# Zero matmuls in the open sums of TensorE, and new orders on all engines, in a four-block token tower on one core

## The chip, the cores and the metric

The kernel runs on one NeuronCore of one Trainium2 chip. Its time is the device time of one launch in microseconds. A NeuronCore has five engines that run side by side, each through its own list of instructions: TensorE (PE, matmuls into PSUM), VectorE (DVE), ScalarE (ACT, table functions such as exp and gelu), GpSimd (POOL), and SyncE (SP, here the issuer of nearly all DMAs). They wait for each other by semaphores, and none of them may overtake in its own list.

## The reference, cut to what matters

64 sequences of 128 token ids go through a tower. Activations are rows of 128 features; all arithmetic is float32.

```python
h = token_block(x)                       # embedding + layer norms, ffn, 8-head attention (second of two layers), ffn
h = h + mamba_block(layernorm(h))        # forward and backward selective scan over time, then ffn and layer norms
h = h + moe(layernorm(h))                # router, 8 experts of gelu(x @ w1[e] + b1[e]) @ w2[e], top 2 combined
h = h + attention(layernorm(h))          # 8 heads
h = h + nibble_alu(layernorm(h))         # rounded features, small relu networks, one-hot outputs
# the scan, for each of 2 directions and each of 16 state indices:
#   h_t = exp(dt_t * A) * h_(t-1) + (dt_t * u_t) * B_t ;  y_t += h_t * C_t
```

## The kernel before

Four sequences form a group: 512 columns (4 x 128 time steps) with the 128 features on partitions. There are 16 groups. On each engine the work of a group is cut into four streams, each a Python generator that stops (`yield`) after every small item:

- `P` (`token`, line 429 in the PE block): the token block and its layer norms, in PSUM banks `bank_p`.
- `A` (`scan`): the selective scan, 32 states of a group (16 forward, 16 backward). For one state ACT computes `decay` (exp), POOL computes `dbu` (dt*u times a row of B), DVE runs two scan instructions into PSUM `states` (L921), two multiplications with the row of C (L927) and two additions into `y_sum` (L932). SP loads the two broadcast rows.
- `C` (`middle`): what follows the scan: the projection back, an ffn, two layer norms, the router, and 8 experts. An expert is 4 times a matmul `h` into `bank_a` (L569), a gelu on ACT, and a matmul `y` that adds to a sum in `bank_b` (L580). The sum is open from the first `y` to the fourth; then DVE takes it out (L1106). The ffn before the experts uses `bank_b` in the same way (L538).
- `D` (`beside`): the preparation of both scan directions of the next group (`pre`), and the last layer of the group two before (`last_layer`), in `bank_c`.

So four groups are in flight at once, at different stages. In which order an engine takes items of the four streams is written out by hand as a string of letters for each engine, in the table `ORDER` (lines 42 to 170), and `drive` (line 348) walks it: each letter takes the next item of that stream. The work inside each stream has a fixed order; only the interleaving is in the strings. Items of a group in the middle of the run repeat the same letters from group to group in the version before (about 218 us apart).

Every f32 matmul of the source is two PE instructions in the profile (1,024 of L569 are 512 matmuls), each with its own weight load. ACT holds one table set at a time: exp and ln share one, gelu, tanh-gelu and silu have one each. `af` (line 697) asks for the exp set when it changes to it (that load has line L701 in the profile); the other loads stand in front of the activation (L705). How often the set changes follows from the letters alone.

Of the kernel before, what the change touches and what calls it, by code (L numbers as in the profile page):

```python
# [14 lines left out]
NSEQ, L, D = 64, 128, 128  # L15
# [34 lines left out]
        "PCCDCCPCCDPPDPCCPCCDPPDCCPPCCPCCCCDCCPCCDPDCCCCDCCDPDPDPCCPCCDDDCCPCCPPCCPPCCPPCCPCCPPDCCDCCDDPCCPDC"  # L50
        "CDCCPPCCDCCDDPCCDPPPCPCCPCDPDCPPCCCCDDCCDCPPDCDDPPDCDDDCDDCDDCDDDDDCCCPCCDPPCCDDPDPCCPDPCCDPCCDCCPCC"
        "DPPDPPPCCCCDCCPCCDPDDPCCCCPCCDCCPDDPDCCCCPCCDPCCPDPPCCPPCCPCCPPDCCDDPCCDCCPDCCDCCPPCCDCCDDPCCDPPPCPC"
        "CPCDPDCPPCCCCDDCCDCPPDCDDPPDCDDDCDDCDDDCDCCCDCCPDDPPCCPDCCDCPCCCPDDPCCPDPCCDCCDCCPCCPDPPDCCPPDCCPDCC"
        "DCCDCCDCPCCCPDDPCCPCCDDDPCCPCCPPPCCPPCCPCCPPDCCDDCCDPCCDCCDCCPPCCDDPDDPPCPCCPPCPCDPCCDCCPPDDPCCDCPPP"
# [1433 lines left out]
```

How the kernel before makes its waits and increments, by code:

```python
    def link(eng, ins, name):  # L298
        eng.wait_ge(s[name], tick(ins, name))
# [17 lines left out]
        @block.tensor  # L318
        def _(pe):
            pe.wait_ge(done["w"], 16)
            pe.wait_ge(done["cols"], 16)
            for i, (name, a, b) in enumerate(FOLD):
                nc.tensor.matmul(A[:, i:i + 1], w(name, a=a, n=128), col(b), start=True, stop=True).then_inc(done["b"], 1)
            pe.wait_ge(done["s"], 1)
            for i in range(2):
                nc.tensor.matmul(B[:, i:i + 1], w(f"wo{i}"), small[:, i:i + 1], start=True, stop=True).then_inc(done["c"], 1)
# [1 line left out]
        @block.vector  # L328
        def _(dve):
            dve.wait_ge(done["b"], len(FOLD))
            nc.vector.tensor_copy(small[:, 0:2], A[:, 0:2]).then_inc(done["s"], 1)
            nc.vector.tensor_copy(COLT[:, COL["q0"]:COL["q0"] + 2], A[:, 2:4])
            b1 = COLT[:, COL["tb1_00"]:COL["tb1_00"] + 2 * NF]
            nc.vector.tensor_tensor(b1, A[:, 4:4 + 2 * NF], b1, ALU.add)
            nc.vector.tensor_scalar(w("tw2_1"), w("tw2_1"), 0.5, None, ALU.mult)
            for name, g in (("wqk0", "tl1s1"), ("wqk1", "tl1s1"), ("wv1", "tl1s1"), ("tw1_0", "tl2s0"), ("tw1_1", "tl2s1")):
                nc.vector.tensor_scalar(w(name), w(name), col(g), None, ALU.mult)
            dve.wait_ge(done["c"], 2)
            nc.vector.tensor_copy(COLT[:, COL["c0"]:COL["c0"] + 2], B[:, 0:2]).then_inc(done["fold"], 1)
            dve.wait_ge(done["fold"], 1)
```

## Time and profile before

| | |
|---|---|
| median of 3 runs | 3891.53 us (3889.09 to 3901.82) |
| the profiled execution's own time | 3896.18 us |
| its span, first to last instruction | 3893.9 us |
| mean granted TensorE clock | 0.887 of full |

The span is what all rows below refer to; 2.3 us lie around it. A row of a group of instructions gives their count, their busy time in all, the mean of one, and the idle time that the engine had just in front of them. Granted clock 1.00 means that TensorE ran at its upper level (2.4 GHz), 0.50 at its lower one (1.2 GHz) in the whole stretch, and values between are mixtures of both.

### The profile page before, as it was taken

The numbers are of one execution on the slowest core, as the hardware profiler recorded it, in microseconds if no ns is written. First come the engines' busy times: TensorE is split into PE (matmuls) and PEld (weight loads), VectorE is DVE, ScalarE is ACT, GpSimd is POOL, SyncE is SP. The second block draws the span as 40 slices with busy tenths as digits, with TensorE's granted clock in tenths as the row PEclk, the third lists the DMA queues.
The fourth block names the chain that finished last, engine by engine and source line by source line (L and its number), as shares of the span: only waits on it lengthen the run. The fifth ranks groups of instructions, "written<-read, shape, count | busy, mean of one in ns | idle before, by whom it ended". The sixth has DMA issues, their size and how long they took to land.

```text
span 3893.9 us, 31221 instructions
## 1 busy us (share of the span) xinstructions
PE 3127.3 (80%) x8728; PEld 1368.3 (35%) x8728; DVE 3420.1 (88%) x4654; ACT 2925.3 (75%) x3806; POOL 1337.2 (34%) x644
## 2 busy tenths in 40 slices
PE   5655878889787788979888888979788887877797
PEld 3231423334343333424343333424343333432232
DVE  1499979999898999999999999999999998999822
ACT  2546887987868888787888878787888879686442
POOL 0254333333323334343433443343433433333200
PEclk8757788989888899989999999989989999888797
DMA  1233333424324243333434342343424333333310
GB/s 63 77 108 96 113 109 92 128 80 135 99 94 118 93 131 95 119 118 109 125 98 123 107 131 94 121 117 109 124 95 126 104 116 104 104 119 104 100 49 11
DMA packets 209022, 404.60 MB, mean 104 GB/s; under 512 B 25936, under 2 KB 34256, under 8 KB 208592
## 3 DMA queue, kind: packets, MB, share of 16 engines
q1 hardware_dynamic: 206800, 398.41, 32.8%
q0 software_dynamic: 2048, 4.20, 1.0%
q8 instruction: 69, 1.13, 0.1%
q14 instruction: 105, 0.86, 0.1%
HBM read 387.57 MB, written 14.94 MB: 103 GB/s over the span
## 4 chain that ended last, share of the span: by engine, by line
PE 37%; DVE 26%; ACT 25%; issue 12%; POOL 0%; DMA 0%; DVEq 0%; ACTq 0%; POOLq 0%
PE bank_a L569 8%; DVE states L921 7%; PE bank_b L580 7%; ACT L705 6%; DVE states L927 6%; ACT decay L705 6%; DVE y_sum L932 3%; ACT L701 3%; ACT tok L705 3%; ACT last L705 3%; ACT middle L705 3%; PE bank_p L478 1%; PE bank_c L397 1%; PE bank_p L421 1%; PE bank_c L640 1%
## 5 line engine op out<-in xcount | busy, mean ns | idle before, releaser
L1199 POOL TENSOR_TENSOR dbu<-dtu,b_rows 128x1024 f32<-128x1024 f32 x512 | 1243.4, 2431 | 2104.1 <-DVE states L921 1823.6
L921 DVE TENSOR_TENSOR_SCAN states<-decay,dbu 128x512 f32<-128x512 f32 x1024 | 1298.7, 1311 | 38.1 <-ACT decay L705 30.5
L705 ACT ACTIVATE decay<-dt,neg_a 128x508 f32<-128x508 f32 x1024 | 659.4, 707 | 64.6 <-DVE states L921 59.0
L705 ACT ACT_TABLE_LOAD x516 | 662.0, 1283 | 47.5 <-PEq L344 16.6
L569 PE MATMUL bank_a<-middle,experts 128*128 128x512 f32 x1024 | 616.2, 687 | 97.1 <-ACT middle L705 88.9
L705 ACT ACTIVATE middle<-bank_a,columns 128x512 f32<-128x512 f32 x608 | 417.8, 687 | 329.6 <-PE bank_a L569 305.4
L927 DVE TENSOR_TENSOR states<-states,c_rows 128x512 f32<-128x512 f32 x960 | 610.8, 679 | 0.3
L932 DVE TENSOR_TENSOR y_sum<-y_sum,states 128x512 f32<-128x512 f32 x960 | 609.9, 674 | 0.2
L580 PE MATMUL bank_b<-middle,experts 128*128 128x512 f32 x1024 | 572.7, 643 | 21.4 <-ACT middle L705 11.8
L705 ACT ACTIVATE last<-bank_c 128x512 f32<-128x512 f32 (+2 forms) x320 | 201.0, 634 | 198.0 <-PE bank_c L617 52.4
L701 ACT ACT_TABLE_LOAD x232 | 297.7, 1283 | 46.0 <-PE bank_p L469 17.0
L580 PEld LDWEIGHTS bank_b<-middle,experts 128*128 128x128 f32 x1024 | 209.2, 208 | 312.0 <-issue 248.1
L569 PEld LDWEIGHTS bank_a<-middle,experts 128*128 128x128 f32 x1024 | 187.5, 209 | 365.5 <-issue 189.5
L705 ACT ACTIVATE tok<-bank_p,columns 128x512 f32<-128x512 f32 x304 | 203.7, 684 | 64.9 <-PE bank_p L421 36.7
L397 PE MATMUL bank_c<-xin,weights 128*128 128x512 f32 x256 | 151.9, 687 | 94.6 <-DVE xin L1018 55.8
L705 ACT ACTIVATE tok<-bank_p 128x512 f32<-128x512 f32 x224 | 132.3, 590 | 100.2 <-PE bank_p L376 47.7
L421 PE MATMUL bank_p<-tok,weights 128*128 128x512 f32 x256 | 153.2, 683 | 56.9 <-DVE tok L896 35.1
L1106 DVE SCALAR_TENSOR_TENSOR middle<-bank_b,columns,comb_rows 128x512 f32<-128x512 f32 x128 | 94.8, 741 | 117.0 <-PE bank_b L580 115.7
L426 PE MATMUL bank_p<-tok,weights 128*128 128x512 f32 x256 | 147.4, 660 | 51.2 <-ACT tok L705 51.1
L478 PEld LDWEIGHTS bank_p<-tok 128*128 128x128 f32 x1024 | 150.0, 218 | 98.1 <-ACT tok L705 64.3
L478 PE MATMUL bank_p<-tok 128*128 128x17 f32 x1024 | 147.8, 279 | 36.3 <-ACT tok L705 36.0
L379 PE MATMUL bank_p<-tok,weights 128*128 128x512 f32 x128 | 83.0, 734 | 58.2 <-ACT tok L705 57.5
(206 smaller groups left out, 3944.7 us busy)
## 6 DMA issues: line engine op xcount, KB each, us to landing
b_rows<-bc_scratch SPq DMA_DIRECT2D x512, 256.0 KB, 3.4
c_rows<-bc_scratch SPq DMA_DIRECT2D x512, 256.0 KB, 3.3
experts<-ew SPq DMA_DIRECT2D x128, 512.0 KB, 3.5
comb_rows<-comb_scratch SPq DMA_DIRECT2D x128, 256.0 KB, 3.8
h_scratch<-tok SPq DMA_DIRECT2D x16, 256.0 KB, 3.3
x_scratch<-xin SPq DMA_DIRECT2D x16, 256.0 KB, 3.8
xr<-x_scratch SPq DMA_DIRECT2D x16, 256.0 KB, 4.9
h<-h_scratch SPq DMA_DIRECT2D x16, 256.0 KB, 5.3
```

Source lines behind the costliest of these rows:

```text
L397: last = mm(bk, w(dn + "in", a=128 * e, n=128), xin[:, :], start=True, stop=(e >= HALVES))
L421: tick(mm(bh, w(w1, a=128 * c, n=128), x, start=True, stop=True), p + "h")
L426: tick(mm(by, w(w2, a=128 * (c - 1), n=128), slots[c - 1], start=(c == 1), stop=(c == NF)), p + "y")
L478: last = mm((P, Q)[hd // 4][:, at:at + 17], ex[:, it % 2, blk(2 * i + j)], va[:, 2 * a + j, hd, :], start=True, stop=True)
L569: tick(mm(A, EW[:, e % 2, 128 * c:128 * c + 128], s_xn, start=True, stop=True), "e_h")
L580: tick(mm(B, EW[:, e % 2, FF + 128 * c:FF + 128 * c + 128], gbuf[:, k % 4], start=(c == 0), stop=(c == NF - 1)), "e_y")
L701: act.preload_act_table_set("natural_log_exp_and_others")
L705: return nc.scalar.activation(out, in_, func, **more)
L921: tick(nc.vector.tensor_tensor_scan(hs[:, h, ::step], da[:, n % DECAYS, h, ::step], dbu[:, n % AHEAD, h, ::step], 0.0, ALU.mult, ALU.add), ...
L927: tick(tt(hs[:, h] if st else y_sum[:, h], hs[:, h], c_rows[:, n % SLOTS], ALU.mult), "a_hc")
L932: tick(tt(y_sum[:, h], y_sum[:, h], hs[:, h], ALU.add), "a_y")
L1199: tick(nc.gpsimd.tensor_tensor(dbu[:, n % AHEAD], dtu[:, k % 2], row, ALU.mult), "a_dbu")
```

## The change

Three things change.

1. The five strings of `ORDER` are replaced by new ones. Counts of P, A, C and D are as before on every engine (PE 753 P, 1,282 C, 801 D; ACT 2,261 letters; DVE 2,823; POOL 546; SP 1,317). The new strings don't repeat from group to group.
2. The string of PE has 1,435 letters `F` besides. Each is one bf16 matmul of 256 columns: weights that are all zero, a moving operand read twice from the first 128 columns of the constant tile `selections`, added (`start=False, stop=False`) to columns 0 to 255 of `bank_b`. Every `F` stands after an item of `C` that leaves a sum in `bank_b` open. They wait for nothing and signal nothing.
3. A tile of zeros takes 256 bytes of each partition; one `memset` on DVE fills it in the set-up. To make room, `neg_a` has no tile of its own, but is computed in place in `weights`.

```diff
 ORDER = {
     "passes": 0,
     "PE": (
-        "PDCPPPPPPPPPPPPCPPPPPPPPPPPPPPPPPPPPPPPPPPPPPPPPPPPDDDPDCPDPDPPDDPDDPPDPPDPPPPPPPPPPPPPPPPPPPPPPPPPP"
+        "PDCPPPPPPPPPPPCPPPPPPPPPPPPPPPPPPPPPPPPPPPPPPPPPPPPDDPDDPCDPDPDDPPDDPPDPPDPPPPPPPPPPPPPPPPPPPPPPPPPP"
+        "PPPPPPPPPPPDDDPDDPDPPDDPPPPPPPPPPPCPCPDDCFFFFFFFFFFFFFFFFFFFCCPFDCCDCCPPFFFFFPPFFFFPPFFFFFCCPCPCPPPC"
...
-    NEGA = sb("neg_a", [128, 2 * HALVES * DS])
+    ZERO = sb("zeros", [128, 128], BF16)
     EW = sb("experts", [128, 2, 2 * FF])
+
+    NEGA = W[:, AT["falog"][0]:AT["falog"][0] + 2 * HALVES * DS]
...
         def _(dve):
+            nc.vector.memset(ZERO[:, :], 0.0)
             dve.wait_ge(done["b"], len(FOLD))
...
-            drive("PE", P=each(token), C=whole(fold, middle), D=beside())
+            def nothing_added():
+                finite = sel("fieldcum").rearrange("p (a t) -> p a t", a=1).to_broadcast([128, 2, 128])
+                for _ in range("".join(ORDER["PE"]).count("F")):
+                    mm(B[:, 0:256].rearrange("p (s t) -> p s t", s=2), ZERO[:, :], finite, start=False, stop=False)
+                    yield
+
+            drive("PE", P=each(token), C=whole(fold, middle), D=beside(), F=nothing_added())
```

What the new strings say when they are counted:

| | before | after |
|---|---|---|
| changes of ACT's table set that the letters cause | 747 | 669 |
| runs of `F` on PE, and the longest | - | 328, 30 |
| `F` in runs of 10 or more | - | 677 in 40 runs |
| `F` from the middle stream of group 15 on | - | 22 |
| DVE items after the last `A` | 52 D, 26 C | 53 D, 26 C |
| scan states issued on POOL before the gathers of groups 2, 3, 4 | 63, 94, 127 | 57, 88, 119 |

## Rows read from the trace of the kernel before

**Rows 1.** The page: busy us, share of the span, instructions; granted clock in fortieths.
```profile
PE 3127.3 (80%) x8728; PEld 1368.3 (35%) x8728; DVE 3420.1 (88%) x4654; ACT 2925.3 (75%) x3806; POOL 1337.2 (34%) x644
PEclk8757788989888899989999999989989999888797
```
**Rows 2.** Windows: head, early, repeating, late, tail; busy us (instructions), granted clock, DMA.
```profile
0.00:162.90 162.90, 103.97 (x293) 55.59 (x294) 24.98 (x55) 53.94 (x70) 17.75 (x27) 0.78 0.20 66
162.90:1380.40 1217.50, 930.02 (x2562) 414.37 (x2561) 1128.56 (x1501) 924.40 (x1198) 460.71 (x216) 0.84 0.35 105
1380.40:2693.90 1313.50, 1110.47 (x3272) 487.84 (x3270) 1272.97 (x1735) 1104.60 (x1437) 499.87 (x240) 0.94 0.37 114
2693.90:3692.40 998.50, 813.95 (x2197) 346.62 (x2197) 936.73 (x1266) 773.97 (x1001) 358.85 (x161) 0.90 0.36 111
3692.40:3893.90 201.50, 168.89 (x409) 63.86 (x408) 56.88 (x103) 68.41 (x102) 0.00 (x0) 0.89 0.09 29
```
**Rows 3.** The same windows for the scans of L921 alone: DVE busy (count), clock.
```profile
162.90:1380.40 1217.50, 441.64 (x352) 0.84 0.35 105
1380.40:2693.90 1313.50, 497.07 (x384) 0.94 0.37 114
2693.90:3692.40 998.50, 359.93 (x288) 0.90 0.36 111
```
**Rows 4.** Timeline: two scans back to back, and two that met a late `dbu`.
```profile
2120.47 2.33 DVE L921 TENSOR_TENSOR_SCAN states<-decay,dbu 128x512 f32<-128x512 f32 x2
2113.60 2.36 POOL L1199 TENSOR_TENSOR dbu<-dtu,b_rows 128x1024 f32<-128x1024 f32 x1
2114.34 3.83 DVE L921 TENSOR_TENSOR_SCAN states<-decay,dbu 128x512 f32<-128x512 f32 x2
```
**Rows 5.** What DVE waited for, us in total, times, longest; 162.9 to 3692.4 us.
```profile
DVE middle L1106 <- PE bank_b L580: 72.6, 36, 15.2
DVE states L921 <- ACT decay L705: 30.5, 9, 12.3
DVE last L947 <- ACT last L705: 16.4, 7, 6.7
```
**Rows 6.** Timeline of PE about 2180 us: a pause, and the matmuls before and behind it.
```profile
2174.60 1.02 PE L376 MATMUL bank_p<-tok,weights 128*128 128x512 f32 x2
2178.03 2.07 PE L379 MATMUL bank_p<-tok,weights 128*128 128x512 f32 x2 [2.41 <-ACT tok L705]
2190.14 1.02 PE L379 MATMUL bank_c<-last,weights 128*128 128x512 f32 x2
2191.00 1.02 PE L538 MATMUL bank_b<-middle,weights 128*128 128x512 f32 x2
```
**Rows 7.** Windows about the same pause: the clock is the value behind the five engines.
```profile
2172.20:2177.70 5.50, 3.42 (x10) 1.06 (x6) 5.50 (x8) 4.71 (x5) 2.36 (x1) 1.00 0.35 126
2177.70:2183.10 5.40, 2.07 (x2) 0.50 (x2) 5.40 (x7) 5.37 (x10) 2.96 (x1) 0.51 0.19 53
```
**Rows 8.** Single lines: durations in ns, min/median/max, of bf16 and f32 matmuls.
```profile
L645 PE MATMUL bank_c<-last,selections x16: 379/389/606, 690.7 to 3866.4; 128*128 128x512 bf16 x16
L538 PE MATMUL bank_b<-middle,weights x128: 592/592/1061, 358.2 to 3717.7; 128*128 128x512 f32 x128
```
**Rows 9.** Groups of the page: both kinds of table load.
```profile
L705 ACT ACT_TABLE_LOAD x516 | 662.0, 1283 | 47.5 <-PEq L344 16.6
L701 ACT ACT_TABLE_LOAD x232 | 297.7, 1283 | 46.0 <-PE bank_p L469 17.0
```
**Rows 10.** Timeline of ACT about 549 us: loads and activations in turn.
```profile
547.62 1.28 ACT L705 ACT_TABLE_LOAD   x1
548.92 0.69 ACT L705 ACTIVATE tok<-bank_p,columns 128x512 f32<-128x512 f32 x1
549.62 1.28 ACT L705 ACT_TABLE_LOAD   x1
```
**Rows 11.** Who waited for whom in the expert loop, us in total, times, longest.
```profile
ACT middle L705 <- PE bank_a L569: 305.4, 222, 5.2
```

More of the change, by code:

```diff
@@ L50 @@
[L50 to L54, printed above, removed]
@@ new lines @@
+        "PPCPCCPCFFFFFCCPCCPCCPCCPCCFFFFFFFFPFFFFFFCCFCCPPCCFCCPPFCCFFFFFFFFFFFFFCCPPCCFCCPFFFCCPFFFFFPFFFFFF"
+        "FFFFFDCCDDPCCDFFCCFFDCCFFFFDFFPFFFFFFFFFPFFFFFFFFFFFFCCDCCPCCDCCPPFFFFFFFFFFFCCPPCCFCCPPFCCFCCPCCPFF"
+        "FPFFFFFFFFFFFFFPCCDDPPFFCCPCCCCPCDCCPPDFCCFFFFFFFFFPPFFFFPPFCCFCDDPCDPCPPCDPPDCPPCDPDDPDCCCPCCPCCPCC"
+        "DCCDFFFPDFFFDDCCFPPDCCDCCPPDCCDDFFFFFFFFFFFFFCCPPFCCDCCPDDCCPDDPFFFCCDCCFFDCCPCDCCCDCCFFFFFFFFFFDFFF"
+        "FFFDCCDCCDCCDCCDCCDPPCCDCCDDPFCCDCCDDPCCDPCCFFDCCFPDPCCCPCPPDDCPFFFFPFFFCCDDFFCCFFDCCFFFFDFPFFFFFFFF"
@@ new lines @@
+        "FPFPFFPFFFFFFFFFDDFFFFFFDFFFFFFCPCPPDDPPCPPCDPDDPDCPPCDPPDDPPCCCPDCCPCCPCCPCCPCCDFFFFFDPDFFFDDCCDFFF"
+        "FFFFFCCPPCCDCCPPDCCDDFFFFDCCPPDCCDCCPDCCPCCDPPDCCCCDCCFCCDCCDDFFDDFFFFFFFFCCDCCDCCDCDCCCDPFFFCCPDDFF"
+        "CCDCCFFFFDFFFPFFFFFFFFFFFFCCPPFCCDCPPDCPPPPCPDCDPCFPPFFFCCPFDCCFFDFFFFFFFFFFFFFFFFFFFFFFFFFFFFFFDDFC"
+        "CPCDCPPCPCPDPPDCDPCDPDDDDCCCPPDCCDDPPDFFPPDFCCDCCPDDPCCPCCDCCPCCPCCDCCDDFFPFFFFFCCDCCPPDCCDCCPCCPDFF"
+        "FFDFFFCCPPCCFFFFFFFFFFFDFFCCPDCCPCPCCDDCFFFFFDDDPFFFCCPCCPCCDCDDCPFDDCCDDFFCCFFDFCCPDPCCFFFFFFFFFFFF"
@@ new lines @@
+        "FCCPPDCCDPCPDCCPDCPPCPCCDPPDFCCPFFFFFFFFFFFFFFFFFFFFFFFFFFDDFFFFDFPCCFFFFPPDDCDCDPPDPCPDCPDDPCPPCPPD"
+        "CCPCPDDFCCDCCPDFFPCCPCDPCCCPDDFFFFFFFCCDCCPCDCCCPPDCCDDFFFFFCCDPPCCDCCPPCCDCCPDPCCFFPDFFFFFFFDPDDFCC"
+        "DCCDCCDCCFCCFCCDDDFFFFFFCCDCCDDPCCDPFCCFFDCCDPCCPCCPCCPPCDDCPPCPDCPDPCFFFFFFFFPCCDPPDFFCCPFFFFFFFFFF"
+        "FFFFFFFFFFFFFFFFDDFFFDFPFCCFFFFPPDDCDCDPPDPCPDCPDDPCPPCPPDCCDDCPPDFCCDCCPDDPDFFFCCPCCPCCPCCDCCDDPDDC"
+        "CPPDCCDCCPPCCDCCPPDCCFFFFFFFFFFFFFFFDFFCCDPFCCPCPDCCCDDDPDFFFFFCCFCCPCDDCCCDCCPDDFFFFPFFFCCDDCCFFDCC"
@@ new lines @@
+        "FPDPCCFFFFFFFFFFFFFFFCCDPCPCCCPPCCDCPCCPCPCPDCCPPCCPCCDFFFFFFFFFFFFFFFFFFFFFFFFFCPDCPPDCPPCPPDDCPDCP"
+        "DDDCCPCPDCCDDPPDDFFPPDCCDDPFDFFPCCPCDPCCCPCCDDFDFFFFPFFFFDCCDPPCCDCCPPCCDCCPPCCDCCPDFCCPFFDPFDFCCDCC"
+        "PFFFFDFFFFCCDCCDCCDCCDCCDCCDFFPFFFPFFFCCDCDDCFFPDCCDDCCFDFFFCCDCCFPDPCCFFFFFFFFFFFFFFFCCDPCPDPPPPCCP"
+        "CPCPPFFFCCPDDFFCCFDFCCFFDFFFFFFFFFFFFFFFFFFFFFFFFFFDDFFFFDPFFCCPPDDPPCPPCDPDCPDCPPDDDCCCPPDCCDDPPDFF"
+        "PDFFCCPCCPCCPCCPCCDDFFFDPFFFFFFFFCCPPDCCDDPPDCCDFFFFCCDPPFCCDCCPDFFPDFPFFFFFFFFFFDFCCPCCDCCCDDCCCDDF"
@@ new lines @@
+        "DFFFFFCCFCCCDDCCCDCCPDDPFFCCDDCCFFDCCFFFFDFFFFPFFFFFFFFFFFCCFPPDCCDPCCPCCPPCCFFFFFFFFFFFFFFFFFFFFCPC"
+        "CPCPDDCPFFFFPPFFFPFFFFCCFDFCCFFDFFFFFFFFFFFFFFFFFFFFFFPFFFFFPPDDCCDFFPPFFDPPDCDDPCDDPCPPCDPPDCPPCDPD"
+        "PCCCPCCPCCPCCDCCFFDPFFFDFFFFFFCCDPPDCCDFFFFFFFFFCCPPDCCDDPPCCDCCPDCCDCPCCCDPFFFCCFCCDPDCCFFFFFFFFPCC"
+        "DCCDCCPCDDCCCDDDFFFFFFFFFFCCFCCDCDDCCCDCCDPFCCDDCCFFDCCFPDPCCFFFFFFFFFFFFCDCCPCPDDCFFFFFFFFFFFFFFCCF"
+        "PPCCFDFFFCCPFFFCPDCPDCPCPPPDDCCDPDDCCCPPDCCDDPPDDPPDCCDCCPDDPCCDCCPPDFFFPPDDCCDPPFFFFCCCCPDFPCCPCCDP"
@@ new lines @@
+        "CPCCDCDFFDFPFFCCFCCDPPCCDPCCPDFFFFFDFFFCCPPFCCFFFFFFFFFFFFFFDFFCCPDCPCPCCDCCDDFFFDDPFFFCCCCPCCDCCDCC"
+        "DCCPDDFPFFFCCDDFFFCCFDFCPCDPPPPCPCPDDCPFFFPFFFFFFFFFFPCCDDPPDPCCDFFFFFFFFFFFFFFFFFFFFFFFFFFFFFFDDFFF"
+        "FDPFFCCFFFPPDDFCDDCPPDCPPCDPDDPCPPCDPPDDPCCCPDFCCDCCPDDPDFFFCCPCCPCCPCCDCCDDPDDCCPPDCCDCCPPCCDCPPDCC"
+        "CFFFFFFFFFFFFFFDFFCCDPFCCPCPDCCCDDDPDFFFFCCFCCPCPDCCCDDFFFFFDDCCDDFFCCPDCCDFFPPCCFFFFFFFFFFFFFFFFFFF"
+        "FFDCCPPCCDCCPPCCFFFFFFFFFFFFFFFFFCCPFFFCPDCCPDCPPCPPFFFFFFCCFFDCCFFFDFFFFFFFFFFFFFFFFFFFFFPFFFFFPPDD"
@@ new lines @@
+        "CCDCPPCPPDCPDCDDPDDCPPDDPCPDDCCDCPPCCDCCPDFFFPDDCCPDPCCPCCDCCDDPFCCDCCPPCCDCCPPDCCDCCDPPCCDCCPFFCCPP"
+        "DDPCCCCDCCDCCDCDCCCDPFFFPFFFFFFCCDCCDDPCCDCCDDPCCDPCCDCCFPDPCCFFFFFFFFFFFFCCDPCPDCCPDDCPPCPCCDPPFCCP"
+        "CCDFFFFFFFFFFFFFFFFFFFFFFFFFFFDDPFFFCDCPPPCPDCPPDDPDCPDDCPPDDDCCCPPDDCCDFPPFDFFFCCDCCPDDPCCPCCPCCPCC"
+        "DCDDPCDFFDCCPPDCCDCCPPCCDCCPPDCCFFFFFFFFFFFFFFDFFFFCCDPCCPCCPCCDCCDDPDDCCFCCFCCDCCDCCDPFFFDDPCCDDFFC"
+        "CFDFCCDPCCPCCPCCPPCDDPPCCPDCPDPCPCCPPCCDPCCDFFFFFFFFFFFFFFFFFFFFFFFFFFFFFFDDPFCDCPPPPCPPCDPDDPDCPPDD"
@@ new lines @@
+        "PCPDDDCCCPPDCCDFPDFFFFPDFCCPCCDCPCDPDFFFFFFDFCCPCCDCCPPDCCDCCPPCCDDFFFFDCCPPDCCDFPFFFCCPFFFFPFFFFFDF"
+        "FFFFFCCDCCDCDCCCDCCDDFFFFFFFFFCCCCDCCDCCDCCDDCCFDDFFCCFDFCCDFFFFFFFFFFFFFFFFCCCCCCDCCDCCCDCDCFDFCCDC"
+        "CFFFFFFFFFFFFFFFFFFFFFFFCCFCDDCDCCCCCCCFCCFCCFCCCCCCDDFDFFFDFCCDCCDCCDCCDCCFDFFFFFDDFCCDCCDCCDCCDDFF"
+        "FFFFFFFFFFFCCDCCFCCDCCDCCDCCFCCDCCFDFFFDFFFCCDCDCCCFFFFFFFFFDFFFCCDCCCDDDCCCDCCDFFFFFFFFFCCDDDDDDDDD"
+        "DDDDCDCDCDDCCDCCDCCDCDDCDCDDCDDCDCDCCCDCCDCCFFFFFFFDCCDCCDCCDCCDCCDCCDCCFCCDCCDCCDCCDFCCFCCCCFCCFCCF"
@@ L75 @@
+        "CCCCFCCFCCFCCCCFCCFCCFCCCCFCCFCCFCDDDDDDDDDDDDDDDDDDDDDDDDDDDDDDDDDDDDD",
         "",
@@ new lines @@
+        "APAAPCDCDCDCADAADPAAPCCCCPAAACPCCPCCPCPAPAAPACDDPPCPCPPAPACAACADCPADCDPAAPCCPCDACDPACPCDAPCPCDDPCCCP"
+        "CCPDAAADCPDCDCPDCDDAAACPCCPDCADAPCDCPDACCCDCDAAACCDCDCDCAAADPCCPACDCPDCDCDCPDCDPCPCPAAAAPCDDCDCPDAAD"
+        "PPAPPAPAPDACDCPACPDAPCPCDADPCPCDPADPCCCPCCPCAPDADADCDDACPCCPDCADACPDCDCPCDCAPADPAACCCCCDADDAADCCCCDC"
+        "AAACPDDCDCPDAADCPCCPPPAPAAPAADCDPCAAPPCPDCPDPADPAAACDCCPCDPAACACPDAPDCCDPDCCDPADAPDCDCPDDAACPCCDCPCC"
+        "PDAACCPDCDPCCAAADCPCDAACPCCPCAPDDADACDCPCCPAADACDDCDCPDCDCPCPCDDPACPACPAAPAACDPPDCPDPPAPAAADCDPACDCP"
@@ new lines @@
+        "CDAPDACPCADPCPCPCDACDCPDACDPCCDDPAAPCCDCCPDCAACDPCDCPCCPDCDPAAPAAACDDCDCCDCCAAACDCDCDPCDCPDAADAACPCC"
+        "PCPAAAAPDCPDCPAAPACDPPDCPDPPAPAAADCDPACDCPCDAPDACPCADPCPCDPCADCDCPDAADDCPCCPCCPDADACPDCDCPCCPDCADAAA"
+        "CPCCPCDPDADAACDCCPCCADAPAACDDCDCPDCDACPCCPCCPAPAAACPACPADDCPPCPCPPAPAAACDCPCDPADCPAACPDADCCDPCDCPDAA"
+        "DPCDPADCDPCCDPCADDPAACPDCDCPCCPCCPDCADPAAACDCPDAACCCDCDCDCAAADPCCPAADCDCDCDCPDCDACPCPPPAPAAACPACAPPC"
+        "PDDCDCPDPADPAAAADCDCPACPDAPCPCDAPCDCDPCCDPADAPDCDCPCCPCAPDDAACPCDPDCACDPCDCPAADAPDPACCCCCDDAADACDCCC"
@@ new lines @@
+        "CADAPACDDCDCPDAADCPCPCCPCAAAAACPDPDCPCPAAAPPAPPCDCPDPDAAAAPCDPDAPCDPCDACDAPCPCDAPCPCDPCCCPCCPDAADACD"
+        "PCDDAACPCDPCDCPCDCDCAPAACCPADCDACPCCCCPDDADAADCCCCDCAACDDCDCPDCDCPDCCAAAAACPCDCPCPDCPACDPADCPPCPPAPA"
+        "PCDAADACDPCCDPADAPCDCPDACDCPDAAPDCDDPACCPACDPCCDPCPACDCPCDCPAAADCPCDAAACPCCPCPDADDAACDCCPCCCADAPACDD"
+        "CDCPDPDPPCCPAAAPAAPCDDPPDPCDPDPAPAAAADCDPACDCPDCAPDACPACDPCPCDPDACCDCPDAADDCPCCPCCPDADACPDCDCPCCPDCA"
+        "DAAACPCCPCDPDADAACDCCPCPAADACDDCDCDPCDAAACPCCPCAAAACPCPDDPACPACAPPAPAPCDCPDPDAAAAPCDCPDCPACAPDCACDPD"
@@ new lines @@
+        "APDCCDPCCDCPDAADCDPDACPCCPDCDCPCCPDCADAACPCDCPCDAPAAPACCCDCDCDCAAADPACCPACDCPDCDCDCPDCDCPCDPDACPACPA"
+        "APAACDPPCDPCPPADPAAACDCPCDPAACPACDPDAPDCCDPDCACDPADCDCPDDAACPCCPCCPDDAACPDCDCPCCPDCADAAACPCCPCCPDADD"
+        "AACDCCCCAADPACDDCDCPDAADCPCCPCPAAAAPDCPDCPAAPACPPCDPCDPPDPAAAACDCPCDPAAPCPACDDPAPDCCDPDCCPDAADCPDCCD"
+        "DPAAPCDCCPDCCPCAADDACPCDPCDAPAAPCCCDCDCADAADCCCCCADAACDDCDCDADCCCCCAAAAADCDCAADCDCDAAACCCDCDAACACACC"
+        "CCCCCCAADACDCDCCDCAAADCDCDCDCDDAAACCDCCDCCCCDADAACCDCDAACCCCDDDCAAADCDADDDDDDCCDCDCDCDCDDCCDCDCDCDCC"
@@ L103 @@
+        "CDCDCCCDCDCDCCDCCCCDCCCCCCCCCCCCCCCCCCDDDDDDDDDDDDDDDDDDDDDDD",
         "",
@@ new lines @@
+        "AAAAPACPCAAAPAAAAACACAAAAAAAAAACAACAAPAAAAAPAAACAACAAAAAAPAAADADADPCDCAAAAAAAAAACACAAAAAACACAAAAAPAA"
+        "AAAAAACACAAPAPACAAAAAAAAAADADADADAPCADACACADCACCCPDCCADAPAPAAACAPDACAADAAAAAAAACACAADADDAADDDADDCAPC"
+        "DADDDADAAAPAADACAACAADADADDADACPCAAAAAACADCDAADAPAAAAACACAAAAAAAAACCDDDDCAAAAAAAAAPAAADAADADADAPAPAD"
+        "AACDAACAAPDCADCACDCCCCAAAPDAAAPACPCAAAPAAAAADADDCDDDCDADAAAADADDDADAACACAADAPAAACADCPAADADDAAADAACAC"
+        "AAADAADADAAPACAACAAAAAAACAACAPAAADADADADACACAAAAAAAAAAPACAAAAAAAAAAADAADPDPDAAAACDAAACAAACADCAPCDCCD"
@@ new lines @@
+        "CCADAAAADAAAAAACPDCDDADDDAPAADDPCACAAAAPDADDDADACACAAAADAAAAAACAACDADADDAAPDAAACACAPAAPADADAAADCPACA"
+        "AAAAAAAAACACADADADADAACCAAACAPAAAAAAAAAADADADPDPAAADAADAAACDAACADPCADCACCCCCAAAADAAAPAAAPCAADPDCDADD"
+        "DPADDACACAAADADDDADAACACAAADAAAACPACADDADPDADAAAAAAACADCDAADAAAPACAACAAAAAACPCAAADADADADAAAACAACAAAA"
+        "AAAAACAAAPAAAAAAAAADADADPDPAADAAADAAACDAACADPCADCACCCCCAADAAAAAAPADADCDPDDDPDCAADAPDCADDDCDAAAAAAAAD"
+        "AACACAAADAADADDADAPACAACAPAAAAAPDADCADCAAAAAAPAAACACAAAAAAADADADADCAACAAACACAAAACAPAAAAAAAAAAAPAPAAA"
@@ new lines @@
+        "ACAAADCDADCDAACPADCCCCCDAAADAADAADAAADAPAAAPCAPCAAAADPDDADDDADDACAACADADDADADCACAAPAAAADAAACPADCDADD"
+        "AADAACAACAAAPADAADADCACPAAAAAAAAACACAAADDADADAACACAAAAAPACAAAAAAAAAAAAADADPDADPAAADAACDAACACPDCACCCD"
+        "CCDAAAAADAAAPAAACPAAPCAAAPDADDAADDDCDDCAADADDDAADAAAACADAAPCAADAPDADDAAAADACACAAAAADADACDCAPAAAAAAAC"
+        "AACAAAAPAADADADADACAACAAAAAAAACACAAAAACAPAAAAAAAAAAAAPADPDADADAADAAADAADPCDAACACADCACCCPCCDAAPAPAAAC"
+        "APAACAAAAAAADADDADDDCDDCADAADDDADPACACAAAADACPCAAAADPDADDAADACAACAAAADAPADADCACAAAAAAACACAAAAAAAAADD"
@@ L167 @@
+        "AAPAAAPAACAAAAAACAACCCDAAADAAAACAAAACAAAAAAAADAAAAAAAAAAAAACACACAAAAAACAAAACAAAAAACAACAAAACCCAAAAAAC"
+        "AAAACADCCCCCDCCCD",
         "",
```

125 lines of the change are left out of this document (32 added, 93 removed).

## The prediction

> **What bounds the kernel now.** I read the page's busy shares first: DVE is busy for 3420.1 us of 3893.9, ACT for 2925.3, PE for 3127.3, and the granted clock varies between 5 and 9 tenths over the run [rows 1]. So three engines are heavily used and DVE is the one that can set the end. Then the windows, cut where DVE's scans begin (162.9 us) and end (3692.4 us) and where the letters repeat from group to group (1380.4 to 2693.9) [rows 2]. The reader is to see there that DVE has its idle time in three places. The head has 162.9 - 25.0 = 138 us and the tail 201.5 - 56.9 = 145 us: single-group chains in which DVE mostly waits. Between them DVE is idle for 1217.5 - 1128.6 = 88.9 us in the early part (7.3%), 1313.5 - 1273.0 = 40.5 us in the repeating part (3.1%) and 998.5 - 936.7 = 61.8 us in the late part (6.2%). That is 191 us, and the granted clock goes with it: 0.84, 0.94, 0.90.
>
> DVE's busy time holds some waiting too. Two scans back to back take 2.33 us, 1.165 each; where `dbu` came late they are booked with 3.83 [rows 4]. At 1.165 the scans of the three parts would take 410, 447 and 336 us instead of 442, 497 and 360 [rows 3]: 106 us in which DVE waited for POOL. So the scans' stretch of 3529.5 us holds 191 + 106 = 297 us that a better order could win, and 3233 us of DVE work that no part of this change touches.
>
> Of the 191 us, the largest named wait is for the experts' sum in `bank_b` with 72.6 us; behind it come ACT's `decay` with 30.5 and ACT's `last` with 16.4 [rows 5]. PE and ACT in turn wait for each other in the expert loop (ACT for `bank_a`: 305.4 us [rows 11]), most of it beside a busy DVE.
>
> **The change part by part.** All on the span of 3893.9 us; the profiled execution's own time is 3896.2, which is 4.6 us above the median of 3891.5.
>
> *The clock.* About 2178 us PE had a pause of 2.4 us; the granted clock of the next 5.4 us was 0.51, the lower level of 1.2 GHz, and the same pair of f32 matmuls took 2.07 us there against 1.02 before and later [rows 6, 7]. A mean of 0.887 means that the lower level held for 2 x 0.113 = 22.6% of the span, 880 us. The `F` matmuls stand in pauses of that kind while a sum in `bank_b` is open. The first such sum is the ffn's of group 0, at 358 us [rows 8], so the head and the first 200 us of scans get none, and from the middle stream of group 15 on there are 22. I take the mean clock between 358 us and the tail to come to what the repeating part shows now, 0.94, or a little more. What that is worth on DVE: if the early and the late part came to the repeating part's idle share of 3.1%, they would lose 88.9 - 37.5 = 51.4 and 61.8 - 30.8 = 31.0 us, 82 us together. The waits that end at PE's `bank_b` are 72.6 of 191 us, and a further 46.9 end at ACT [rows 5], which itself often waits for PE; so not all of the 82 is the clock's. I take half, -41 us. Its bounds are 0 (all those waits have another last cause) and -82.
>
> *The 1,435 zero matmuls.* No row shows one. The nearest is bf16 with 512 columns, 379 ns at the least; f32 instructions of 512 columns last 592 ns [rows 8], though two of them stand 0.43 us apart (a pair each 0.86 us from 2190.14 to 2191.00 [rows 6]), so about 162 ns of such a duration overlap with the next. 379 - 162 = 217 ns for 512 columns gives 109 ns for 256 at the upper level, by the same rows twice that, 217 ns, at the lower. All together 156 us, at most 311 us. PE is idle for 3893.9 - 3127.3 = 767 us now [rows 1], and real matmuls get shorter when the clock rises, by up to a half in the stretches that change level, so PE as a whole has room: its busy time should stay near 3130 us. But an `F` doesn't ask whether the next real matmul could start. If a gap of the plan is not there in the run, the `F` that stand in it are a delay, up to 30 x 109 = 3.3 us in the longest run. I take +6 us on the end (4% of 156); the lower bound is 0, the upper one is the 677 in runs of ten and more at 109 ns, 74 us.
>
> The Trainium skill says that TensorE pulls only weight loads ahead and keeps matmuls in program order ("TensorE: Matmul & The Clock Gate", Part 2, step 1). By that rule none of the zero matmuls can give way, which speaks against the change; the price if it bites is the rival below, and no row of before contradicts it.
>
> *The table loads.* The new letters of ACT cause 669 changes of the table set instead of 747 (the trace has 516 + 232 = 748 loads, so counting letters works [rows 9]). From the start of a load to its activation it takes 1.30 us [rows 10], so 78 fewer take 101 us off ACT's 2925. Where load and activation alternate, each of ACT's items takes 2.0 us [rows 10], and PE and DVE wait behind it. In the repeating part ACT has 1313.5 - 1104.6 = 209 us free [rows 2], so most of the saving there shortens ACT's waits and not the group. I take -5 us; bounds 0 and -47, all the DVE waits named for ACT [rows 5].
>
> The Trainium skill gives a table switch another 1.38 us of drain, 2.66 us in all ("ScalarE: Activation LUTs", What ACT_TABLE_LOAD costs). By it the 78 would be worth 207 us of ACT and my term -10. The trace disagrees: an activation begins 1.30 us after its load began, with nothing between [rows 10], and the row decides.
>
> *The new interleaving.* Everything else moves by a few places. The skew between streams is as before to within a few items, and so is what DVE has left after the last scan (79 items against 78), so I expect the tail at its 200 us and the head at its 163, each within 10. The gathers on POOL and the stores and id loads on SP that go with them come 6 or 7 states earlier in groups 2 to 4: a gather that is issued at another point still holds POOL for four DMA issues, during which `dbu` waits. Its cost sits in the 106 us hidden in the scans. I take 0, bounded by -20 and +20. The new strings of DVE don't repeat, and the repeating part's 3.1% could rise: at the early part's 7.3% its 1313.5 us would cost 55 us more. I take 0 here as well and keep 55 for the rivals.
>
> *The rest.* The memset of zeros stands on DVE in the set-up, where DVE waits for weights; `neg_a` in place changes an address. Both 0; without that cover the memset is one short instruction.
>
> Sum: -41 + 6 - 5 = -40 us, 3896.2 - 40 = 3856 for an execution like the profiled one, and 4.6 less for the median: 3852 us.
>
> **The rivals.**
>
> *The zero matmuls get in the way* (slower). Place: the expert loop, where they stand behind a `y` and in front of the next `h`, which ACT's gelu and then DVE's take-out of the sum depend on. For it: PE keeps its order, and ACT waits for `bank_a` for 305 us already [rows 11]. Against it: DVE waits only 72.6 us on that loop in 3529 [rows 5], so there is slack between. Price: if the 677 of the long runs land with two thirds of their 74 us, +49, and the clock gives a quarter of its 82, -21: +28, 3920 us. It decides as soon as more than about 41 + 5 = 46 us of the 156 reach DVE.
>
> *DVE-bound anyway* (no change). For it: the repeating part is at 3.1% idle with the clock at 0.94 [rows 2]; there is little left to win, and an order without repetition loses some of it. With a third of the 55 us lost (+18), a third of the 82 won (-27), and +6 for `F`: -3, so 3889.
>
> *The clock doesn't rise*: the zero matmuls run, but the lower level comes in the stretches where no sum is open. Then only the order and the table loads count: -5, with 0 to +6 for `F`, and a mean clock still within 0.01 of 0.887: 3892. A difference within 0.3% (12 us) is about what three runs of this kernel can't tell from no change.
>
> *Much better order*: the plan wins half of all 297 us, -148: 3744. Nothing in the rows speaks for it but the room itself.
>
> **How the numbers follow.** Forecast (gain of 12 to 90 us) 0.62, zero matmuls in the way 0.15, DVE-bound anyway 0.12, clock doesn't rise 0.07, much better order 0.04. Faster by over 0.3%: 0.62 + 0.04 and a small share of the two middle cases, 0.68. Slower by over 0.3%: 0.15 and a share of the same, 0.18. Within: 0.14. The low end is the forecast with the full 82 us and the early gap of ACT closed as well, 3892 - 97 = 3795. The high end keeps most of the slower rival out but its beginning, 3908; a tenth lies above, a little under a tenth below.
>
> **What would show it.** Right: a mean clock of 0.93 or more with the rise after 358 us and none in the head; PE's busy time near 3130 with 1,435 more instructions; about 670 table loads; DVE's idle share between first and last scan down from 5.4% (191 of 3529.5) to about 4.3%; the wait for `bank_b` down from 72.6. Wrong: a clock at 0.94 with DVE's waits unchanged (the clock was never the price), a new wait of ACT or DVE behind PE with `F` in front of the awaited matmul, or more than 106 us hidden in the scans.

## The result and the profile after

The changed kernel takes 3933.19 us (median of 5 runs, 3921.97 to 3942.17) against 3891.53 before: a ratio of 1.0103 with a 95% interval of 1.0077 to 1.0130. It is 1% slower, where 1% faster was forecast. The profiled execution took 3942.17 us, its span is 3940.4, and its mean clock 0.890 against 0.887.

The page after, as in [rows 1] (busy time, share, instructions) and [rows 9] (table loads), and the group of the zero matmuls, which is new:

```profile
PE 3275.7 (83%) x10147; PEld 1518.9 (39%) x10163; DVE 3418.2 (87%) x4655; ACT 2823.4 (72%) x3728; POOL 1354.0 (34%) x644
...
L728 ACT ACT_TABLE_LOAD x482 | 618.4, 1283 | 52.8 <-PE bank_a L586 25.9
...
L724 ACT ACT_TABLE_LOAD x188 | 241.2, 1283 | 22.8 <-PE bank_b L513 6.0
...
L710 PE MATMUL bank_b<-selections,zeros 128*128 128x256 bf16 x1435 | 220.7, 282 | 0.0
```

DVE's busy time is the same (3418.2 against 3420.1 us), ACT has its 101.9 us less, and the whole loss is idle time of DVE: 3940.4 - 3418.2 = 522.2 us against 473.8. Where it came in is seen when both spans are cut at the start of the scans of group 5 and of group 14, so that each stretch holds the same groups: the first five, the nine whose letters repeated (or nearly so) before, and the last two with the tail. The windows of before, then of the changed kernel; after the stretch and its length come PE, PEld, DVE, ACT and POOL busy, then the clock:

```profile
0.00:1269.80 1269.80, 946.59 (x2589) 430.52 (x2590) 1043.82 (x1399) 892.68 (x1148) 439.57 (x227) 0.83 0.33 101
1269.80:3252.00 1982.20, 1666.97 (x4873) 731.52 (x4872) 1909.85 (x2601) 1654.97 (x2150) 749.31 (x356) 0.93 0.37 113
3252.00:3893.90 641.90, 513.73 (x1268) 206.25 (x1266) 466.45 (x655) 377.66 (x510) 148.30 (x61) 0.87 0.26 83
```

```profile
0.00:1238.80 1238.80, 982.67 (x3005) 470.13 (x3009) 1031.60 (x1400) 849.68 (x1114) 443.44 (x227) 0.85 0.34 103
1238.80:3311.30 2072.50, 1778.86 (x5690) 829.10 (x5698) 1924.20 (x2601) 1622.20 (x2128) 763.34 (x356) 0.91 0.34 108
3311.30:3940.40 629.10, 514.16 (x1455) 219.71 (x1459) 462.41 (x654) 351.51 (x487) 147.22 (x61) 0.89 0.26 83
```

The first five groups are 31.0 us shorter and the end 12.8, but the nine groups between take 90.3 us more: 230 us each instead of 220. DVE's idle time there went from 72.4 to 148.3 us. And the clock, which was to rise, fell in just these nine groups from 0.93 to 0.91, with over 800 zero matmuls in them.

### The profile page after: what moved, and what is told of

It reads as the page before. It is cut to its first block, busy times and chain, and to the rows that moved or that the text cites. A ratio compares the mean times of both kernels' runs of the same rounds, so it can differ in the third digit from the quotient of the medians.

```text
span 3940.4 us, 33981 instructions
## 1 busy us (share of the span) xinstructions
PE 3275.7 (83%) x10147; PEld 1518.9 (39%) x10163; DVE 3418.2 (87%) x4655; ACT 2823.4 (72%) x3728; POOL 1354.0 (34%) x644
## 4 chain that ended last, share of the span: by engine, by line
PE 37%; DVE 25%; ACT 22%; issue 13%; DMA 1%; POOL 1%; DVEq 0%; ACTq 0%; SPq 0%; another core or an unknown queue 0%; POOLq 0%
DVE states L944 8%; PE bank_a L586 7%; DVE states L950 5%; ACT decay L728 5%; PE bank_b L597 5%; ACT L728 5%; DVE y_sum L955 3%; ACT middle L728 3%; ACT L724 3%; ACT last L728 3%; ACT tok L728 3%; PE bank_p L495 2%; PE bank_p L486 2%; PE bank_c L617 1%; PE bank_p L438 1%
## 5 line engine op out<-in xcount | busy, mean ns | idle before, releaser
L944 DVE TENSOR_TENSOR_SCAN states<-decay,dbu 128x512 f32<-128x512 f32 x1024 | 1271.1, 1284 | 25.6 <-ACT decay L728 22.1
L728 ACT ACTIVATE decay<-dt,weights 128x508 f32<-128x508 f32 x1024 | 656.3, 707 | 51.5 <-DVE states L944 48.8
L586 PE MATMUL bank_a<-middle,experts 128*128 128x512 f32 x1024 | 586.9, 657 | 112.5 <-ACT middle L728 106.7
L597 PE MATMUL bank_b<-middle,experts 128*128 128x512 f32 x1024 | 555.2, 625 | 22.3 <-DVE middle L1129 11.5
L710 PE MATMUL bank_b<-selections,zeros 128*128 128x256 bf16 x1435 | 220.7, 282 | 0.0
L710 PEld LDWEIGHTS bank_b<-selections,zeros 128*128 128x128 bf16 x1435 | 141.5, 101 | 162.8 <-issue 148.2
L495 PEld LDWEIGHTS bank_p<-tok 128*128 128x128 f32 x1024 | 164.9, 237 | 94.2 <-ACT tok L728 54.3
L438 PE MATMUL bank_p<-tok,weights 128*128 128x512 f32 x256 | 153.4, 684 | 42.7 <-DVE tok L919 33.6
L495 PE MATMUL bank_p<-tok 128*128 128x17 f32 x1024 | 161.7, 293 | 28.7 <-ACT tok L728 28.6
L414 PE MATMUL bank_c<-xin,weights 128*128 128x512 f32 x256 | 136.7, 628 | 19.7 <-DVE xin L1041 8.6
```

What stands on the lines that cost most here:

```text
L414: last = mm(bk, w(dn + "in", a=128 * e, n=128), xin[:, :], start=True, stop=(e >= HALVES))
L438: tick(mm(bh, w(w1, a=128 * c, n=128), x, start=True, stop=True), p + "h")
L495: last = mm((P, Q)[hd // 4][:, at:at + 17], ex[:, it % 2, blk(2 * i + j)], va[:, 2 * a + j, hd, :], start=True, stop=True)
L586: tick(mm(A, EW[:, e % 2, 128 * c:128 * c + 128], s_xn, start=True, stop=True), "e_h")
L597: tick(mm(B, EW[:, e % 2, FF + 128 * c:FF + 128 * c + 128], gbuf[:, k % 4], start=(c == 0), stop=(c == NF - 1)), "e_y")
L710: mm(B[:, 0:256].rearrange("p (s t) -> p s t", s=2), ZERO[:, :], finite, start=False, stop=False)
```

## The experiments

"Before" was run beside each; its medians were 3892 to 3896, and each ratio is against the runs beside. Windows and waits come from one profiled execution of each kernel. Executions of one kernel differ by up to 35 us (3887 to 3923 for 512 columns), so a few microseconds between two stretches mean little.

**The two parts apart.** First the new strings without the zero matmuls, then the zero matmuls in the old strings, in two doses. For these the PE string of before was kept and letters `F` were put in front of those items before which the trace of before shows PE idle while a sum in `bank_b` is open (220 gaps).

```diff
# the changed kernel without zero matmuls: every F taken out of ORDER["PE"]
-        "PPPPPPPPPPPDDDPDDPDPPDDPPPPPPPPPPPCPCPDDCFFFFFFFFFFFFFFFFFFFCCPFDCCDCCPPFFFFFPPFFFFPPFFFFFCCPCPCPPPC"
+        "PPPPPPPPPPPDDDPDDPDPPDDPPPPPPPPPPPCPCPDDCCCPDCCDCCPPPPPPCCPCPCPPPC"
...
# old orders (in words): the strings of before on all engines, F added in ORDER["PE"], 2,692 or 1,385 of them
```

> The changed kernel with the 1,435 zero matmuls left out of PE's string and nothing else. Theory 1 (the new interleaving is what costs; the zero matmuls are nearly free): it stays 0.8 to 1.3% above before, 3920 to 3942 us. Rival 2 (the zero matmuls delay real ones): back to before or better, 3860 to 3895. Rival 3 (the zero matmuls help by the clock and hide an even worse order): above the changed kernel, 3945 to 3990, with a mean clock of 0.87 or less against 0.89.

Measured: 3971.67 us, ratio 1.0190 (1.0177 to 1.0204), clock 0.858. The new strings alone are 1.9% slower than before, and the zero matmuls make that 38.5 us better (0.87% by the two ratios, 34 us). The number matched theory 3, against which I had held theory 1, though both say that the new strings are what costs.

> The letters of before on all engines, and zero matmuls put in only where the trace of before shows PE idle while a sum in bank_b is open, for 0.8 of each such gap (2,692 of them in 220 gaps). Theory 1: DVE sets the end and few of its waits are the clock's, so the time is that of before within 0.5% although the mean clock rises to 0.91 to 0.94. Rival 2 (they delay real matmuls): 1% or more above before. Rival 3 (the clock is worth time): 1% or more below before, 3850 or less.

Measured: 3900.81 us, ratio 1.0017 (1.0006 to 1.0028), clock 0.924, both as theory 1 had it.

> As the run with 2,692 zero matmuls in the old order, but for 0.43 of each gap, which makes about as many as the changed kernel has. Theory 1: within 0.4% of before, mean clock between 0.89 and 0.93. Rival 2: about half the loss of the run with 2,692. Rival 3: about half its gain.

Measured (the kernel has 1,385 of them): 3891.74 us, ratio 0.9988 (0.9978 to 0.9997), clock 0.912. So the old order's clock rises by 0.025 to 0.037 and its time stays within 0.2%. The nine groups, windows of the run with 1,385 and then of the one with 2,692:

```profile
1266.50:3250.00 1983.50, 1714.89 (x5666) 793.23 (x5674) 1909.36 (x2601) 1654.66 (x2150) 747.09 (x356) 0.96 0.36 113
...
1268.20:3271.40 2003.20, 1794.37 (x6428) 863.01 (x6436) 1907.02 (x2601) 1655.92 (x2150) 751.39 (x356) 0.96 0.36 112
```

1983.5 us at a clock of 0.96 against 1982.2 at 0.93: DVE is at 96% there, and the higher clock brings no net gain. With 2,692 the nine groups take 21 us more at the same clock of 0.96, and the last two groups with the tail 16 us less (626.0 against 641.9), so the whole hides two effects of opposite sign.

Most of the 21 us seem to come from one place. In front of one of PE's items (L376 before, L406 here) the wait for DVE is an item of its own, and the `F` were put between that wait and the matmul. There they don't fill the pause but stand behind it:

```profile
2195.16 5.30 PE L723 MATMUL bank_b<-selections,zeros 128*128 128x256 bf16 x24 [4.17 <-DVE dt L990]
2200.25 1.09 PE L406 MATMUL bank_c<-middle,weights 128*128 128x512 f32 x2
```

The matmul that could have started at 2195.16 starts at 2200.25. This happens seven times in the nine groups, about 5 us each with 2,692 zero matmuls and 2.8 to 3.4 us each with 1,385. It reaches DVE: its wait for ACT's `last` in the nine groups, before and with 2,692, is

```profile
DVE last L898 <- ACT last L705: 3.2, 5, 1.1
DVE last L934 <- ACT last L741: 21.5, 7, 3.8
```

So rival 2 is at work in both runs, beside theory 1, and they show a gain from the clock less this delay, not the worth of the clock alone. No run has these zero matmuls in front of the wait, so how much of the 21 us they are stays open. In the changed kernel no zero matmul has such a pause just in front of it.

**How wide.** The same 1,435 places, with 16, 512 and twice 512 columns instead of 256.

```diff
-                    mm(B[:, 0:256].rearrange("p (s t) -> p s t", s=2), ZERO[:, :], finite, start=False, stop=False)
+                    mm(B.rearrange("p (s t) -> p s t", s=4), ZERO[:, :], finite, start=False, stop=False)   # 512; finite four times wide
# 16 columns: B[:, 0:16]; 1,024: the line of 512 twice
```

> The changed kernel with each zero matmul 16 columns wide instead of 256: the same 1,435 instructions and weight loads in the same places, with hardly any streaming. Theory 1 (what the zero matmuls gave back came from the clock, and it goes with the time that they keep the array busy): near the new order without them, 3955 to 3975 us, mean clock 0.855 to 0.87. Rival (they help by holding back the matmul behind them, or by loading its weights, not by the clock): near the changed kernel, 3925 to 3940 with a clock of 0.87 or less.

Measured: 3954.06 us (ratio 1.0155), clock 0.864. Just better than expected, at 18 us below none at all (14 by the ratios). That is over a third of what 256 columns give, while the clock rose by 0.006 of 0.032. The rival, near 3933, is out, but a part of the gain may have another cause than the clock; no run separates it.

> The changed kernel with each zero matmul 512 columns wide instead of 256, so 217 ns instead of 109 at the upper level, 155 us more of PE in all. Theory 1: their pauses hold most of it, so at most 15 us slower than the changed kernel. Rival 2: 30 us slower or more, since their delay doubles. Rival 3: faster than the changed kernel by 5 us or more with a higher clock.

Measured: 3905.63 us, ratio 1.0032 (1.0016 to 1.0048), clock 0.910. Rival 3 again: 155 us more of booked zero matmuls, and the kernel is 28 us faster.

> The changed kernel with two 512-column zero matmuls for each one: 0.43 us in the place of 0.109, 623 us of PE in all. Theory 1 (the new order is slower because it was made for matmuls at the upper level and pays for each one at the lower; what is left are pauses without an open sum): the clock rises a little more, to 0.92 or 0.93, but the longest runs, 30 x 0.43 = 13 us, now outlast their pauses, so the gain turns: 3915 to 3990. Rival (still more clock, still faster): below 3895.

Measured: 3921.00 us (ratio 1.0071), clock 0.928. The gain turns, as expected: the highest clock of the new orders, and 15 us slower than 512 columns. Here the zero matmuls hold up the real ones: PE had a pause behind only 9 of the 40 longest runs, against all 40 with 256 and with 512 columns.

In the new order, up to 512 columns, more clock and less time go together, though not in proportion: none 0.858 and 3971.7, 16 columns 0.864 and 3954.1, 256 columns 0.890 and 3933.2, 512 columns 0.910 and 3905.6. But the clock doesn't explain what the nine groups lost. Their windows with 512 columns, and with none:

```profile
1222.90:3279.30 2056.40, 1829.33 (x5690) 816.54 (x5697) 1929.02 (x2601) 1622.41 (x2129) 762.85 (x356) 0.94 0.35 109
```

```profile
1246.30:3331.50 2085.20, 1719.96 (x4872) 763.46 (x4879) 1925.37 (x2601) 1622.26 (x2128) 759.46 (x356) 0.88 0.34 108
```

At 0.94, a hundredth above what before had, they still take 2056 us against 1982. Of the 103 us between 2085 and 1982 the zero matmuls of 512 columns give back 29, and 74 are left that no difference in the mean clock accounts for.

**Which zero matmuls.** Only the 677 in runs of ten or more, and only the other 758.

```diff
# the edits of the string, in effect
+ long runs:  ORDER["PE"] = re.sub("F+", lambda m: m[0] if len(m[0]) >= 10 else "", ORDER["PE"])
+ short runs: ORDER["PE"] = re.sub("F{10,}", "", ORDER["PE"])
```

> The changed kernel with only the 677 zero matmuls that stand in runs of ten or more (40 runs). Theory 1 (the clock gives back the time, and it is the long pauses that lower it): most of the 38 us between no zero matmuls (3972) and all of them (3933) is kept, 3935 to 3952, mean clock 0.875 or more. Rival (the short runs, between the matmuls of an expert, matter more): 3955 or more.

Measured: 3946.34 us (3930.81 to 3961.07), ratio 1.0138 (1.0109 to 1.0167), clock 0.880, as theory 1 had it.

> The changed kernel with only the 758 zero matmuls in runs of fewer than ten (288 runs). Theory 1: 3950 to 3970, mean clock 0.87 or less. Rival: 3935 to 3950.

Measured: 3938.02 us (3931.42 to 3947.18), ratio 1.0114 (1.0094 to 1.0134), clock 0.879: the rival's time, not theory 1's. Either half gives the same clock and most of the gain, and the intervals overlap. My preference for the long pauses is not borne out; that short runs matter more isn't either.

**The orders spliced.** The strings can be cut where the trace of before stands at a given time, since what has started by then on all engines needs nothing that hasn't. Each stream's items are numbered; the first part takes those that were started by 1270 us, in the new interleaving, the last part those not started by 3252 us, and between stand the letters of before.

```diff
# in effect, for each engine: X, Y = items per stream started by 1270 and by 3252 us in the trace of before
+ spliced  = [k for k in new if number(k) <= X[k]] + old[n1:n2] + [k for k in new if number(k) > Y[k]]
#   with F: every F of the new parts doubled, old[n1:n2] with the F of the run with 1,385
+ reversed = old[:n1] + [k for k in new if X[k] < number(k) <= Y[k]] + old[n2:]
```

> All five strings put together from both versions, cut where the trace of before stands at 1270 and 3252 us: the new interleaving for the first five and the last two groups, that of before for the nine repeating ones between, with twice the new version's zero matmuls in the new parts and those of the run with 1,385 between. Theory 1 (the new order loses in the groups that repeated, 218 us each before and 228 after, and wins in the first groups and the last two when the clock is up): 3820 to 3860 us. Rival (its loss is in the clock everywhere, its gain nowhere): 3885 to 3910.

Measured: 3838.44 us (3834.24 to 3849.51), ratio 0.9861 (0.9843 to 0.9879), clock 0.920. It beats both kernels, by 1.4% and by 2.4%. It has 2,034 zero matmuls: those of the new parts stand there twice, and the middle has those of the old order with 1,385. So its ends differ from the changed kernel's in the dose as well. Its windows:

```profile
0.00:1220.70 1220.70, 998.34 (x3413) 496.59 (x3417) 1030.88 (x1401) 847.63 (x1113) 443.26 (x227) 0.87 0.34 104
1220.70:3206.60 1985.90, 1718.43 (x5667) 795.19 (x5675) 1908.23 (x2602) 1654.75 (x2150) 746.68 (x356) 0.95 0.37 113
3206.60:3839.90 633.30, 530.32 (x1668) 239.71 (x1670) 459.68 (x654) 358.50 (x495) 147.74 (x62) 0.91 0.26 84
```

The nine groups are back at 1986 us. The first five groups are 49 us shorter than before and the end 9, against 31 and 13 in the changed kernel with single zero matmuls.

> The same spliced strings without any zero matmul. Theory 1: the new parts pay for the lower clock, 20 to 40 us slower than with them, 3850 to 3890. Rival: no difference to the spliced version with them, within 8 us.

Measured: 3900.98 us, ratio 1.0014 (1.0003 to 1.0026), clock 0.878. Worse than expected: without zero matmuls the spliced order is no better than before, so here they are worth 62.5 us, more than the 20 to 40 of theory 1, in part perhaps because they stand twice in the new parts. Its windows:

```profile
0.00:1241.50 1241.50, 948.52 (x2585) 433.24 (x2589) 1035.57 (x1401) 847.81 (x1113) 442.67 (x227) 0.82 0.33 103
1241.50:3232.40 1990.90, 1673.86 (x4865) 737.13 (x4873) 1905.05 (x2601) 1654.60 (x2150) 748.62 (x356) 0.93 0.36 112
3232.40:3893.20 660.80, 526.29 (x1264) 214.67 (x1266) 459.25 (x655) 358.95 (x495) 147.14 (x61) 0.84 0.25 80
```

The old middle differs by 5 us and the new parts by 20.8 and 27.5: the zero matmuls are worth most where the new interleaving stands. Not there alone: the old end gained 16 us from 2,692 of them. And 660.8 us for the end are more than before (641.9) and than the new order without zero matmuls (636.0), so some of the 27.5 us makes good a loss that came with the splice and is not explained.

> The complement of the spliced version: the letters of before for the first five and the last two groups, the new interleaving (with its own 818 zero matmuls) for the nine groups that repeated. Theory 1 (all of the loss sits in the new interleaving of these nine groups): slower than the changed kernel, 3935 to 3985, as it has the loss of the middle and not the gain of the ends. Rival (the loss lay in how the new first groups hand over to the middle): 3890 to 3920.

Measured: 3984.91 us, ratio 1.0242 (1.0220 to 1.0264), clock 0.882. It lies at the very edge of theory 1's range. It is the slowest with zero matmuls at their width of 256, and its nine groups alone do it (its ends take 1271.1 and 643.7 us, as before):

```profile
1271.10:3333.80 2062.70, 1767.37 (x5691) 819.21 (x5689) 1927.87 (x2601) 1617.09 (x2121) 762.00 (x356) 0.92 0.35 109
```

> The same without any zero matmul. Theory 1 (the new middle pays for the lower clock, the old one doesn't): 10 to 30 us slower than with them. Rival (only the new ends are sensitive to the clock): within 8 us of the run with them.

Measured: 4007.33 us, ratio 1.0295 (1.0274 to 1.0315), clock 0.864: 22.4 us slower than with them, as expected.

**What the nine groups wait for.** The waits of PE in them, before and in the new order without zero matmuls (who waited for whom, us in total, times, longest):

```profile
PE bank_a L569 <- ACT middle L705: 43.3, 52, 2.2
PE bank_p L379 <- ACT tok L705: 36.3, 18, 3.2
PE bank_p L426 <- ACT tok L705: 33.6, 8, 4.2
...
PE bank_c L376 <- DVE dt L954: 24.9, 7, 4.2
```

```profile
PE bank_a L586 <- ACT middle L728: 79.5, 50, 7.9
PE bank_c L393 <- DVE dt L977: 54.9, 6, 13.1
PE bank_c L663 <- DVE last L1185: 29.5, 7, 7.2
```

Before, no pause of PE in these groups was over 4.6 us (L376 and L393 are the same line of the source). In the new order 19 are over 5 us, and the longest takes 13.1. The pauses in front of L393 and L663 end with DVE. My reading is that DVE has the awaited item too late in its own string, and that ACT and then DVE run out of `bank_a` and `bank_b` results while PE stands; no run tests it. The waits of DVE in the nine groups of the changed kernel are

```profile
DVE middle L1129 <- PE bank_b L597: 25.4, 17, 5.7
DVE states L944 <- ACT decay L728: 17.6, 10, 5.5
DVE middle L919 <- ACT middle L728: 16.9, 3, 9.4
DVE last L1150 <- PE bank_c L617: 11.5, 8, 3.7
```

where the first was 14.4 and the second 2.5 us before. They are many and of different lines; no single misplaced item stands out, and I did not look for the letters that would have to move. Which of them cost the time stays open.

## Why the prediction was wrong

**The failed step is "The new interleaving": "I take 0 here as well and keep 55 for the rivals".** The new strings alone cost 3971.7 - 3891.5 = 80 us (76 against the before beside them), against a term of 0 and -5 for their table loads. In the nine groups it is 103 us without zero matmuls and 90 with them. The price that I had set aside was about right: 7.3% of idle time, which was 55 us for the six groups that I looked at, would be 78 for these nine; idle was 148.3 of 2072.5 us, 7.2% (7.7% without zero matmuls), and DVE's booked time grew by 14 us besides. What failed is to enter it with 0. The ground for the 0 was "everything else moves by a few places", and the strings say otherwise when places are counted: on PE an item stands 9 places from its old one in the median, a tenth of them over 30 and the furthest 60; on DVE 4 in the median and 63 at most. The spliced orders show that the interleaving within these nine groups is what makes the difference between about 4% and over 7% of idle time in them; the counts of letters and the skew at the end didn't show it.

**The clock.** The size was nearly right: -41 and +6 for the zero matmuls' delay were forecast, and between the new order with and without them lie -38.5 us, of which 16 columns gave 18 with almost no clock. What was wrong is its baseline. I set it against the order of before, where zero matmuls bring no net gain (-0.1% and +0.2% for +0.025 and +0.037), some of them standing behind a wait, and reasoned that early and late parts have a low clock *and* much idle time. That the one makes the other was not shown; both may come from having few items ready. The mean clock came to 0.89 and not to 0.93 or more, because the new order by itself lowers it to 0.858; the rise by the zero matmuls is 0.032.

**The signs that I had named.** DVE's idle share between its first and last scan was to fall from 5.4% to 4.3% and rose to 6.6% (235.5 of 3569.9 us). The wait for `bank_b` did fall as forecast, from 72.6 us, but others came that were not there, here between the first and last scan:

```profile
DVE middle L1129 <- PE bank_b L597: 48.9, 31, 6.3
DVE last L1150 <- PE bank_c L617: 28.4, 18, 4.3
```

PE's busy time was to stay near 3130 us and is 3275.7: it is 3181.0 without zero matmuls, and their 220.7 us are only in part made up by shorter real ones. More than the 106 us hidden in the scans would have been a sign against me, and it didn't come: the scans are booked with 1271.1 us against 1298.7, so about 78 us are hidden there, while DVE's other instructions are booked with 26 us more. The low end of my range used 97 us, of which 82 were the clock's; no row gives the other 15.

**The price of a zero matmul.** 109 ns was derived from f32 and bf16 rows [rows 6, 8]. Ten in a row in the changed kernel:

```profile
2623.48 1.25 PE L710 MATMUL bank_b<-selections,zeros 128*128 128x256 bf16 x10
```

The last takes about 0.27 us to its end, the nine starts before it (1.25 - 0.27) / 9 = 0.109 us. The 40 longest runs were all followed by a pause. Of the 288 short ones 148 were not; they hold 256 zero matmuls, at most 28 us of PE. Without any zero matmul the kernel is slower, so the rival of zero matmuls in the way is out as the main cause at this width; it comes true at 1,024 columns, and behind a wait in the old order. The Trainium skill's rule that matmuls keep their order ("TensorE: Matmul & The Clock Gate", Part 2, step 1) fits the traces and costs little as long as the pause is there. With 2,692 of them L406 stood 5.1 us behind 24 zero matmuls at 2195.16 us though its wait was over, and the 15 us lost from 512 to 1,024 columns at a higher clock fit the rule too.

**The table loads.** 482 + 188 = 670 loads, as counted from the letters, and 101.9 us less of ACT's busy time, 100.1 of them the loads' own, 1.28 us for each of the 78. The drain that the Trainium skill adds ("ScalarE: Activation LUTs", What ACT_TABLE_LOAD costs) would be idle time, which this figure can't show; against it speak the rows of before in which activations and loads follow each other within 0.02 us [rows 10]. What the fewer loads are worth can't be told from the order that brought them.

**Head, tail, DVE-bound.** Head 160.0 us (163 expected); after the last scan come 210.5 us, where before had 203.8 by the same cut. The rival "DVE-bound anyway" had the right mechanism, less to win where the old order repeats and a loss there without repetition, but it took 18 us for the loss where 103 was due.
